# Scan steps taken in pairs, x statistics on ScalarE, the residual on ScalarE and GpSimd

## Chip, cores and metric

The kernel runs on one core of one Trainium2 chip. The metric is the device time of one execution in microseconds; the core has five engines that run their own instruction streams: TensorE (PE), VectorE (DVE), ScalarE (ACT), GpSimd (POOL) and SyncE (SP, which here only issues DMAs).

## The reference

One block of a gated cross-attention model, batch 4, 256 tokens, width 256, all in float32: a selective scan over a context, gated by the normalised x and added to x, then a mixture of 8 experts with 2 shared ones.

```python
# mixer: ctx (4,256,128) -> 256 channels, 16 states a channel
x_  = conv4(in_proj_w @ ctx); u = silu(x_ + conv_b)
dt, Bm, Cm = split(x_proj_w @ u); delta = softplus(dt_proj_w @ dt + dt_proj_b)
for t in range(256):                       # state: (b, 256, 16)
    state = state * exp(delta[t] * A) + (delta[t] * u[t]) * Bm[t]
    y[t] = sum_n state[n] * Cm[t, n]
y = (y + D * u) * silu(layernorm(x))
x = x + tanh(g_xattn) * y
# feed-forward: 2 shared experts and top 2 of 8, 176 wide each
h = layernorm(x)
x = x + tanh(g_ffn) * (shared(h) + 2.5 * sum_top2 w_e * expert_e(h))
```

## The kernel before, in words

**Tiles and steps.** A tile is 128 tokens of one batch entry: 8 tiles, numbered by `b * 2 + half`. The scan runs with channels on the partitions and tokens along the free dimension, in 64 steps of 128x512 elements: a step holds two states, two halves of the channels, 128 tokens; 8 steps make a tile. For each step `m`:
- GpSimd's `times_b(m)` (line 1021, product at 1035) makes `dbu` = delta*u times row B, into a ring of 3.
- ScalarE's `exps(m)` (673, 687) makes the decays in PSUM `psA`, a ring of 2, four instructions.
- VectorE's `scan:m` (927) runs the recurrence from `psA` and `dbu` into PSUM `psH[m % 2]`.
- VectorE's `prod:m` (937) multiplies the states with row C (`cc`, from DRAM) into `prod`, a ring of 3.
- GpSimd's `prod:m` (1083) adds it to the tile's sum `acc`. Tile 0's products are summed by TensorE instead (595).
The second half of a batch entry continues the first: `keep_ends` (915) copies each step's last column, `carry` (1058) multiplies it with the decay, `fix` (1066) adds it to the first column of `dbu` for the second half's step.

**From a tile's sum to the feed-forward.** For tiles 0 to 3 `y_sum` (TensorE) and `gate_y` (962, VectorE) give y; for tiles 4 to 7 GpSimd does it with `fold`, `fold2` and `gate_y` (1088, 1092, 1100). `to_tokens` (622) transposes on TensorE into PSUM `psD`; `residual` (970, VectorE) forms x2 = psD * gate + x in one instruction; `stats` and `variance` (VectorE 978, 984; GpSimd 1119 to 1125), `norm` (799, ScalarE), `to_features` (630, TensorE) and its copy give the tile's features. Then ten units a tile: `up` on TensorE (658, 662), `gate` on ScalarE (815) and VectorE (1009), `mul` (847, 851), `turn` and `hidden`, and `down` (534) in four groups, with `finish` (1016) last. `up:k` waits for `mul:k-2`.

**The gate of y** needs the normalised x: `z_stats` (VectorE 945, 948: bn_stats and bn_aggr; GpSimd 1106 to 1112), `z_norm` and `z_gate`.

**Order.** Every engine follows a list of tasks written out by hand (`ORDER`); nothing overtakes in a list, and semaphores tie the lists. SyncE's list issues the C rows (`rows_c`, 4 steps each), the B rows (`dt`) and, between steps 2 and 3 of the C rows, the weights (`fetch`). The B rows of batch entry 1, needed from step 16 on, are issued behind the weights.

## Time and profile before

| | |
|---|---|
| Time, median of 3 runs | 245.17 us (244.73 to 245.34) |
| Profiled execution, its own time | 245.45 us |
| Its span in the profile | 243.7 us |
| Busy: PE, DVE, ACT, POOL | 210.8, 204.2, 166.5, 185.6 us |
| Granted TensorE clock, mean | 0.965 |

The profile takes one execution. A group's mean is the duration of one instruction; where instructions of an engine follow each other they overlap a little, so that the distance between their starts is shorter than the duration. Busy time says nothing of whether an engine sets the end: for that the view by stretches and the chain of waits are read together.

### The profile page before, as it was taken

The numbers are of one execution on the slowest core, as the hardware profiler recorded it, in microseconds if no ns is written. First come the engines' busy times: TensorE is split into PE (matmuls) and PEld (weight loads), VectorE is DVE, ScalarE is ACT, GpSimd is POOL, SyncE is SP. The second block draws the span as 40 slices with busy tenths as digits, with TensorE's granted clock in tenths as the row PEclk, the third lists the DMA queues.
The fourth block names the chain that finished last, engine by engine and source line by source line (L and its number), as shares of the span: only waits on it lengthen the run. The fifth ranks groups of instructions, "written<-read, shape, count | busy, mean of one in ns | idle before, by whom it ended". The sixth has DMA issues, their size and how long they took to land.

```text
span 243.7 us, 3658 instructions
## 1 busy us (share of the span) xinstructions
PE 210.8 (87%) x854; PEld 146.8 (60%) x854; DVE 204.2 (84%) x499; ACT 166.5 (68%) x502; POOL 185.6 (76%) x227
## 2 busy tenths in 40 slices
PE   8819862958898876789997999999999999999995
PEld 4307541724566653457564767577777677676784
DVE  1887989989999999999999999999998898655320
ACT  4697998995989958767678998566674751433220
POOL 0486798999999999999999999999999767200000
PEclk9965998599999999999999999999999999999999
DMA  6687899697820320023173031203000000000000
GB/s 181 211 235 182 266 435 356 161 360 205 343 85 8 108 86 0 23 65 90 48 318 94 0 89 52 57 0 87 24 0 22 3 1 3 22 0 0 0 24 22
DMA packets 26965, 25.97 MB, mean 107 GB/s; under 512 B 1080, under 2 KB 25920, under 8 KB 26304
## 3 DMA queue, kind: packets, MB, share of 16 engines
q1 hardware_dynamic: 26656, 25.59, 32.6%
q10 hardware_dynamic: 288, 0.16, 0.2%
q8 instruction: 7, 0.11, 0.2%
q14 instruction: 14, 0.11, 0.1%
HBM read 24.56 MB, written 1.18 MB: 106 GB/s over the span
## 4 chain that ended last, share of the span: by engine, by line
PE 38%; POOL 27%; issue 13%; DMA 9%; SPq 9%; ACT 1%; DVE 1%; POOLq 0%; DVEq 0%; ACTq 0%
PE psU L662 17%; POOL acc L1083 14%; PE psD L534 12%; POOL dbu L1035 8%; DMA brows<-xdbl 6%; SPq L499 4%; DMA bb<-brows 3%; PE psM L640 3%; PE psH L541 2%; SPq L489 2%; PE psU L658 1%; POOL rs L1121 1%; SPq L492 1%; POOL dbu L1066 1%; ACT psA L687 1%
## 5 line engine op out<-in xcount | busy, mean ns | idle before, releaser
L662 PE MATMUL psU<-wup,hnT 128*128 128x352 f32 x288 | 95.2, 466 | 7.9 <-DVE hcat L851 4.3
L1035 POOL TENSOR_TENSOR dbu<-du,bb 128x512 f32<-128x512 f32 x64 | 81.5, 1290 | 4.5 <-DVE psH L927 4.0
L687 ACT ACTIVATE psA<-delta,aneg 128x127 f32<-128x127 f32 x256 | 78.1, 359 | 2.8 <-DVE psH L927 2.6
L927 DVE TENSOR_TENSOR_SCAN psH<-psA,dbu 128x512 f32<-128x512 f32 x64 | 76.7, 1219 | 2.2 <-POOL dbu L1066 1.1
L662 PEld LDWEIGHTS psU<-wup,hnT 128*128 128x128 f32 x288 | 51.6, 190 | 35.6 <-DVE hcat L851 8.8
L1083 POOL TENSOR_TENSOR acc<-acc,prod 128x512 f32<-128x512 f32 x42 | 53.6, 1275 | 4.4 <-DVE prod L937 3.0
L815 ACT ACTIVATE tg<-psU 128x176 f32<-128x176 f32 x80 | 25.0, 315 | 46.6 <-PE psU L662 46.0
L534 PE MATMUL psD<-wdn,hT 128*128 128x256 f32 x224 | 52.1, 379 | 0.0
L534 PEld LDWEIGHTS psD<-wdn,hT 128*128 128x128 f32 x224 | 41.8, 190 | 7.4
L937 DVE TENSOR_TENSOR prod<-psH,cc 128x512 f32<-128x512 f32 x64 | 42.0, 679 | 2.6 <-DMA cc<-brows 1.5
L1009 DVE SCALAR_TENSOR_TENSOR ag<-tg,psU 128x176 f32<-128x176 f32 x80 | 25.6, 330 | 15.0 <-ACT tg L815 14.5
L851 DVE SCALAR_TENSOR_TENSOR hcat<-psU,wtok,ag 128x176 f32<-128x176 f32 x64 | 24.1, 394 | 0.7
L822 ACT COPY hT<-psM 128x512 f32<-128x512 f32 (+1 forms) x32 | 16.1, 502 | 6.5 <-PE psM L640 5.9
L565 PE MATMUL psM<-ctx_sb,wk 128*128 128x256 f32 (+3 forms) x48 | 16.3, 513 | 4.2 <-DVE dnc L906 4.2
L640 PE MATMUL psM<-ident,hcat 128*128 128x128 f32 x112 | 17.6, 274 | 1.7 <-DVE hcat L851 0.9
L640 PEld LDWEIGHTS psM<-ident,hcat 128*128 128x128 f32 x112 | 13.7, 140 | 8.6 <-issue 4.4
L565 PEld LDWEIGHTS psM<-ctx_sb,wk 128*128 128x128 f32 x48 | 12.7, 270 | 7.4 <-DVE dnc L906 4.7
L658 PE MATMUL psU<-wup,hnT 128*128 128x360 f32 x32 | 11.2, 472 | 2.1 <-ACT hnT L807 2.1
L1016 DVE SCALAR_TENSOR_TENSOR outb<-psD,gates,x_sb 128x256 f32<-128x256 f32 x8 | 3.8, 476 | 7.6 <-PE psD L534 7.5
L595 PE MATMUL psD<-prod,ident 128*128 128x256 f32 x32 | 7.9, 389 | 2.4 <-DVE prod L937 2.4
L1044 POOL TENSOR_TENSOR wk<-taps,win 128x1024 f32<-128x1024 f32 x1 | 2.4, 2351 | 8.8 <-DMA taps<-in_w_taps 8.8
L1083 POOL TENSOR_TENSOR acc<-prod 128x512 f32<-128x512 f32 x7 | 8.9, 1272 | 0.0
(110 smaller groups left out, 217.1 us busy)
## 6 DMA issues: line engine op xcount, KB each, us to landing
cc<-brows SPq DMA_DIRECT2D x16, 512.0 KB, 3.9
bb<-brows SPq DMA_DIRECT2D x3, 2048.0 KB, 7.5
wup<-in_w_up SPq DMA_DIRECT2D x1, 1760.0 KB, 13.7
wdn<-in_w_down SPq DMA_DIRECT2D x1, 1664.0 KB, 16.7
wup<-in_w_up SPq DMA_DIRECT2D x1, 1408.0 KB, 8.5
x_sb<-in_x SPq DMA_DIRECT2D x4, 256.0 KB, 6.0
bb<-brows SPq DMA_DIRECT2D x1, 1024.0 KB, 6.0
out<-outb SPq DMA_DIRECT2D x8, 128.0 KB, 1.7
```

The lines of the kernel that those rows point to most:

```text
L534: last = pe.matmul(psD[:, 0:D], hT[0:m, g % HT_RING, c:c + P], wdn[0:m, f, :], start=(f == 0), stop=(f == FB - 1))
L565: last = pe.matmul(dst[:, h, back:], wk[:, DC - 1 - back, h * P:(h + 1) * P], ctx_sb[:, b, 0:L - back], start=(back == 0), stop=(back == D ...
L640: last = pe.transpose(psM[0:m, c:c + P], hcat[:, t % 2, f * P:f * P + m], ident[:, :])
L662: last = pe.matmul(dst, hnT[:, b % 2, k, lh * P:(lh + 1) * P], wup[:, j - 1, k, :], start=(k == 0), stop=(k == KT - 1))
L687: last = act.activation(dst[:, j, h, 1:], delta[:, b % 2, h, l0 + 1:l1], ACT.Exp, scale=aneg[:, h * DS + s0 + j:h * DS + s0 + j + 1])
L815: act.activation(tg[:, i % 2, :], psU[:, i % 2, 0:FF], ACT.Tanh, scale=0.5).then_inc(s_tanh, 1)
L851: last = dve.scalar_tensor_tensor(dst, up, wtok[:, b % 2, lh, j - 2:j - 1], ag[:, unit % 2, :], ALU.mult, ALU.mult)
L927: dve.tensor_tensor_scan(psH[:, i % 2], psA[:, i % DA_RING], dbu[:, i % DBU_RING], 0.0, ALU.mult, ALU.add).then_inc(s_scan, 1)
L937: dve.tensor_tensor(tile(prod[:, i % PROD_RING], i), tile(psH[:, i % 2], i), c.unsqueeze(2).broadcast_to([P, ns, EH, l1 - l0]), ALU.mult). ...
L1009: dve.scalar_tensor_tensor(ag[:, i % 2, :], tg[:, i % 2, :], 1.0, psU[:, i % 2, 0:FF], ALU.add, ALU.mult).then_inc(s_ag, 1)
L1035: pool.tensor_tensor(tile(dbu[:, m % DBU_RING], m), du[:, b % 2, :, l0:l1].unsqueeze(1).broadcast_to(shape), bb[:, b % 2, s0:s0 + ns, l0:l ...
L1083: pool.tensor_tensor(acc[:, total % 2], before, prod[:, i % PROD_RING], ALU.add).then_inc(s_add, 1)
```

## The change

Four things change, and the order of all five lists with them (SyncE's stays as it is).

- **Pairs.** `dbu`, `prod` and `acc` hold two steps a slot. One GpSimd product makes `dbu` for two steps (steps 0 and 1 singly), one VectorE product multiplies two steps' states (steps 62 and 63 singly), `keep_ends` and `fix` take two steps. The scans themselves and the decays stay single. A tile's sum is now: 1024 elements (first two pairs), 1024 (third pair), the upper half folded onto the lower (512), and two adds of 512 for the last pair.
- **x statistics.** `z_sum` (Copy with a sum as side output) and `z_square` (Square of x minus its mean, with a sum) on ScalarE, two instructions each for a batch entry, each followed by a wait for its own end; `z_mean` (one) and `z_stats` (three instead of four) on GpSimd.
- **Residual.** ScalarE copies `psD` times the gate into `ytok` in SBUF, GpSimd adds x; VectorE's instruction is gone.
- **Order.** Among others `gate_y:0` moves from behind `scan:11` to between `scan:8` and `scan:9`, and `z_stats:2` and `:3` of GpSimd move from before step 7 to steps 41 and 55.

```diff
 DA_RING, DBU_RING, PROD_RING, HT_RING = 2, 3, 3, 4
+PAIR = 2
...
+SINGLE_DBU = (0, 1)
+SINGLE_PROD = (STEPS - 2, STEPS - 1)
+def steps_of(m, single):
+    return (m, m + 1) if m in single else (m // PAIR * PAIR, m // PAIR * PAIR + PAIR)
...
     "ScalarE": """
+        load:0 project_out:0 z_sum:0 project_out:1 tanh_u:0 z_square:0 skip:0 xproj_out:0 tanh_u:1 dt_out:0
+        soft_exp:0 log_1:0 xproj_out:1 soft_log:0 z_sum:1 first:0 scan:0 dt_out:1 scan:1 soft_exp:1 log_1:1
+        scan:2 soft_log:1 z_norm:0 scan:3 scan:4 z_gate:0 project_out:2 z_square:1 tanh_u:2 scan:5 scan:6
...
     "GpSimd": """
+        z_mean:0 z_stats:0 load:0 first:0 scan:0 z_mean:1 scan:1 scan:3 scan:5 z_stats:1 scan:7 carry:0 fix:8
+        scan:9 fix:10 scan:11 carry:1 residual:0 scan:13 fix:12 fix:14 variance:0 delta0:2 delta1:2 prod:11
+        delta2:2 prod:13 scan:15 z_mean:2 prod:15 scan:17 scan:19 scan:21 scan:23 residual:1 carry:2 prod:19
...
+        carry:4 prod:35 fix:40 z_stats:2 residual:3 prod:37 variance:3 fold:4 scan:41 prod:39 fix:42 fold2:4
+        carry:5 gate_y:4 scan:43 residual:4 scan:45 fix:44 delta0:4 fix:46 delta1:4 prod:43 delta2:4 prod:45
+        variance:4 fold:5 scan:47 prod:47 fold2:5 gate_y:5 z_mean:3 scan:49 residual:5 scan:51 scan:53 z_stats:3
...
+                elif task == "z_sum":
+                    for h in range(LH):
+                        c = i * LH + h
+                        act.activation(zscrap[:, :], x_sb[:, i, h, :], ACT.Copy, accum_out=zsum[:, c:c + 1]).then_inc(s_zsum, 1)
+                        act.wait_ge(s_zsum, c + 1)
+                elif task == "z_square":
+                    act.wait_ge(s_zneg, i + 1)
+                    for h in range(LH):
+                        c = i * LH + h
+                        act.activation(zscrap[:, :], x_sb[:, i, h, :], ACT.Square, bias=zneg[:, c:c + 1],
+                                       accum_out=zsq[:, c:c + 1]).then_inc(s_zsq, 1)
+                        act.wait_ge(s_zsq, c + 1)
...
+                elif task == "residual":
+                    act.wait_ge(s_yT, i + 1)
+                    if i >= 2:
+                        act.wait_ge(s_x2, i - 1)
+                    act.activation(ytok[:, i % 2, :], psD[:, 0:D], ACT.Copy, scale=gates[:, 0:1]).then_inc(s_ytok, 1)
...
-                    if i >= PROD_RING:
-                        dve.wait_ge(*added(i - PROD_RING))
+                    if m0 >= PAIR * PROD_RING:
+                        dve.wait_ge(*added(i // PAIR * PAIR - PAIR * PROD_RING + PAIR - 1))
...
-                elif task == "z_stats":
-                    for h in range(LH):
-                        dve.bn_stats(zst[:, i * LH + h, :], x_sb[:, i, h, :]).then_inc(s_zst, 1)
...
-                elif task == "residual":
-                    dve.wait_ge(s_yT, i + 1)
-                    dve.scalar_tensor_tensor(x2[:, b, h].rearrange("p (k d) -> p k d", k=EH), psB, gates[:, 0:1],
-                                             x_sb[:, b, h].rearrange("p (k d) -> p k d", k=EH), ALU.mult,
-                                             ALU.add).then_inc(s_x2, 1)
...
-                if m >= DBU_RING:
-                    pool.wait_ge(s_scan, m - DBU_RING + 1)
+                if m >= PAIR * DBU_RING:
+                    pool.wait_ge(s_scan, m - PAIR * DBU_RING + PAIR)
...
+                    if k == 1:
+                        pool.tensor_tensor(whole, part(prod, PROD_RING, m0 - PAIR, m0), part(prod, PROD_RING, m0, m1),
+                                           ALU.add).then_inc(s_add, 1)
+                    elif k == 2:
+                        pool.wait_ge(*added(m0 - 1))
+                        pool.tensor_tensor(whole, whole, part(prod, PROD_RING, m0, m1), ALU.add).then_inc(s_add, 1)
+                        pool.wait_ge(*added(i))
+                        pool.tensor_tensor(whole[:, 0:W], whole[:, 0:W], whole[:, W:], ALU.add).then_inc(s_add, 1)
+                    else:
+                        for m in range(m0, m1):
+                            pool.wait_ge(*(added(m - 1) if m % PAIR else folded(t)))
+                            pool.tensor_tensor(whole[:, 0:W], whole[:, 0:W], part(prod, PROD_RING, m, m + 1),
+                                               ALU.add).then_inc(s_add, 1)
...
+                elif task == "residual":
+                    pool.wait_ge(s_ytok, i + 1)
+                    pool.tensor_tensor(x2[:, b, h], ytok[:, i % 2, :], x_sb[:, b, h], ALU.add).then_inc(s_x2, 1)
```

## Rows read from the trace of the kernel before

**Rows 1.** The page, busy us and share of the span of each engine.
```profile
PE 210.8 (87%) x854; PEld 146.8 (60%) x854; DVE 204.2 (84%) x499; ACT 166.5 (68%) x502; POOL 185.6 (76%) x227
```

**Rows 2.** Windows: stretch, its length, then busy us of PE, PEld, DVE, ACT, POOL.
```profile
15.60:55.90 40.30, 27.10 (x88) 19.37 (x89) 36.18 (x69) 36.46 (x104) 35.83 (x46) 0.81 0.89 292
55.90:157.40 101.50, 89.48 (x365) 60.10 (x363) 97.90 (x232) 81.57 (x249) 99.55 (x114) 1.00 0.30 97
157.40:241.00 83.60, 83.45 (x360) 61.66 (x360) 60.34 (x163) 38.65 (x125) 44.76 (x56) 1.00 0.04 14
```

**Rows 3.** Chain of waits, start us, us, what, around 157 us.
```profile
156.66 0.73 POOL yg L1100
...
157.53 0.41 PE psD L622 x2
```

**Rows 4.** Timeline of GpSimd, start us, us (a run's, if xN), what.
```profile
9.22 2.35 POOL L1044 TENSOR_TENSOR wk<-taps,win 128x1024 f32<-128x1024 f32 x1 [8.79 <-DMA taps<-in_w_taps]
...
29.25 0.22 POOL L1106 TENSOR_SCALAR zve<-zmv 128x2 f32<-128x2 f32 x1
...
30.82 1.26 POOL L1035 TENSOR_TENSOR dbu<-du,bb 128x512 f32<-128x512 f32 x1
...
55.95 3.73 POOL L1035 TENSOR_TENSOR dbu<-du,bb 128x512 f32<-128x512 f32 x3
...
93.48 0.52 POOL L1066 TENSOR_TENSOR dbu<-dbu,carry 128x4 f32<-128x4 f32 x3
...
156.66 0.72 POOL L1100 TENSOR_TENSOR yg<-acc,sz 128x256 f32<-128x256 f32 x1
...
165.76 2.69 POOL L1083 TENSOR_TENSOR acc<-acc,prod 128x512 f32<-128x512 f32 x2
```

**Rows 5.** Groups, VectorE and GpSimd: instructions, busy us, mean ns, idle before.
```profile
L937 DVE TENSOR_TENSOR prod<-psH,cc 128x512 f32<-128x512 f32 x64 | 42.0, 679 | 2.6 <-DMA cc<-brows 1.5 <-POOL acc L1083 0.9 <-issue 0.2
L915 DVE COPY ends<-psH 128x4 f32<-128x4 f32 x32 | 4.3, 149 | 0.0
L970 DVE SCALAR_TENSOR_TENSOR x_sb<-psD,gates,x_sb 128x256 f32<-128x256 f32 x8 | 3.8, 473 | 0.7 <-PE psD L622 0.7
L1035 POOL TENSOR_TENSOR dbu<-du,bb 128x512 f32<-128x512 f32 x64 | 81.5, 1290 | 4.5 <-DVE psH L927 4.0 <-DVE du L451 0.5
```

**Rows 6.** Groups on ScalarE, same columns.
```profile
L788 ACT ACTIVATE zn<-x_sb,znb,zrs 128x256 f32<-128x256 f32 x8 | 4.3, 590 | 0.0
L752 ACT ACT_TABLE_LOAD x3 | 3.8, 1283 | 0.1
L807 ACT COPY hnT<-psD 128x256 f32<-128x256 f32 x8 | 3.0, 371 | 0.9 <-PE psD L630 0.9
L810 ACT ACTIVATE psU<-psU 128x8 f32<-128x8 f32 x8 | 1.3, 157 | 4.0 <-PE psU L658 4.0
```

**Rows 7.** SyncE's issue of x's first block, landings of x, ScalarE's waits before 20 us.
```profile
2.44 0.43 SPq L462 DMA_DIRECT2D x_sb<-in_x  x1
...
DMA to landing us min/median/max: 3.7/6.0/6.1
...
ACT psM L715 <- DVE xh L889: 0.8, 1, 0.8
...
ACT uD L764 <- DVE u L899: 0.5, 1, 0.5
ACT xdbl L724 <- PE psM L575: 0.5, 1, 0.5
```

**Rows 8.** Chain of waits: the B rows of batch entry 1.
```profile
38.97 8.13 DMA brows<-xdbl
...
47.12 7.46 DMA bb<-brows
```

**Rows 9.** Chain of waits: `to_tokens:7` and `to_features:7` on TensorE.
```profile
208.40 0.22 PE psD L622 x2
...
213.13 0.31 PE psD L630 x2
```

More of the change, by code:

```diff
@@ L177 @@
+        gate:78 gate:79 hidden:30 hidden:31
     """,
     "VectorE": """
[L179 to L182 removed]
@@ L188 @@
-        keep_ends:22 log_2:3 variance:1 mul:8 mul:9 prod:21 prod:22 scan:23 keep_ends:23 prod:23 z_gate:1
-        scan:24 scan:25 finish:0 prod:24 prod:25 scan:26 scan:27 prod:26 prod:27 gate:10 route:1 mul:10 gate:11
-        gate_y:2 mul:11 scan:28 silu_u:4 prod:28 gate:12 gate:13 mul:12 mul:13 scan:29 scan:30 gate:14 prod:29
-        gate:15 mul:14 mul:15 scan:31 residual:2 gate:16 prod:30 mul:16 stats:2 prod:31 scan:32 gate:17 mul:17
-        variance:2 prod:32 scan:33 gate:18 gate:19 prod:33 keep_ends:32 keep_ends:33 gate_y:3 mul:18 mul:19
@@ L198 @@
-        prod:44 scan:45 scan:46 gate:32 gate:33 mul:32 stats:4 mul:33 prod:45 prod:46 gate:34 variance:4 mul:34
-        scan:47 gate:35 mul:35 prod:47 gate:36 finish:2 mul:36 scan:48 gate:37 mul:37 gate:38 mul:38
-        keep_ends:48 scan:49 gate:39 prod:48 mul:39 gate:40 route:4 mul:40 gate:41 mul:41 residual:5 scan:50
-        gate:42 stats:5 mul:42 gate:43 variance:5 mul:43 prod:49 keep_ends:49 z_gate:3 scan:51 prod:50 gate:44
-        gate:45 keep_ends:50 mul:44 mul:45 keep_ends:51 prod:51 scan:52 scan:53 keep_ends:52 gate:46
@@ new lines @@
+        scan:23 variance:1 keep_ends:23 prod:23 scan:24 scan:25 finish:0 prod:25 z_gate:1 scan:26 scan:27
+        prod:27 gate:10 route:1 mul:10 gate:11 gate_y:2 mul:11 scan:28 scan:29 gate:12 gate:13 mul:12 mul:13
+        prod:29 silu_u:4 scan:30 gate:14 gate:15 mul:14 mul:15 scan:31 prod:31 gate:16 gate:17 stats:2 mul:16
+        variance:2 mul:17 scan:32 scan:33 prod:33 gate_y:3 keep_ends:33 gate:18 gate:19 mul:18 mul:19 scan:34
+        scan:35 gate:20 route:2 mul:20 keep_ends:35 gate:21 prod:35 mul:21 scan:36 scan:37 gate:22 gate:23
```

309 lines of the change are left out of this document (152 added, 157 removed).

## Prediction

> **What bounds the kernel now.** I read three views in this order. The page's busy line [rows 1] shows no single full engine: PE 87%, DVE 84%, POOL 76% of the span. The windows [rows 2] show why an average misleads: from 15.6 to 55.9 us ScalarE, VectorE and GpSimd are all about 90% busy; from 55.9 to 157.4 GpSimd is busy 99.55 of 101.5 us, VectorE 97.9, while TensorE is busy only 89.5; from 157.4 to 241.0 TensorE is busy 83.45 of 83.6 us and the rest waits for it. The chain of waits [rows 3] gives the hinge: GpSimd's `gate_y:5` (starts 156.66), then `to_tokens:5` on TensorE (157.53), then nothing but TensorE up to the last `finish` at 241.0. TensorE's tasks behind `to_tokens:5` are the same in both orders, so the end moves with the end of `gate_y:5` (157.38), unless TensorE meets a new hole behind it. GpSimd sets that moment: its work from step 16's product (55.95) to `gate_y:5` is back to back [rows 4].
>
> **Price of GpSimd work.** Starts, not durations, give the cost of queued instructions. Three `dbu` products of 512 take 3.73 us, the last lasting about 1.28, so one costs (3.73-1.28)/2 = 1.23. Three `fix` of 4 elements take 0.52, 0.15 to 0.16 each. That is 0.155 us fixed and (1.227-0.155)/508 = 2.11 ns an element: 256 elements cost 0.69, 1024 cost 2.31 (the `wk` product of 1024 lasted 2.35) [rows 4]. A pair joined saves 2x1.227-2.31 = 0.147 us, only 6%. An instruction that needs its direct predecessor's result costs 0.1 to 0.2 more (two such adds took 2.69, where two free ones would take 1.23+1.28 = 2.51) [rows 4].
>
> **GpSimd from step 16 to `gate_y:5`, part by part.** Both orders hold the same steps here.
> - Products: 34 single ones become 17 pairs, 17x0.147 = -2.5.
> - Sums: tiles 2 to 5 go from 7 adds of 512 (8.59) to two of 1024 and three of 512 (8.30), 4x0.29 = -1.2; but two adds a tile now follow their own predecessor, nine in all (with tile 1's last), 9x0.15 = +1.35. Together +0.2 (from -1.2 to +0.6).
> - `fix`: 16 become 8, 8x0.155 = -1.2.
> - The residual's add is new here: `residual:1` to `residual:4`, 4x0.69 = +2.8.
> - `z_mean:2` and `z_stats:2` move in from the first stretch. The four-instruction `z_stats` took 1.57 from start to start [rows 4], three take about 1.4 with z_mean 0.2: +1.6.
> Sum: -2.5+0.2-1.2+2.8+1.6 = +0.9. The bound engine gets no lighter.
>
> The Trainium skill (GPSIMD Engine Reference, section 4.1 Engine selection) says that a two-input elementwise operation belongs on VectorE and costs about twice as much on GpSimd. The trace agrees in size: 0.69 against 0.47. By that rule alone the residual's move speaks against this change.
>
> **What it gives back.** GpSimd's own costs add up to about 100.0 us here (64 instructions of 512 by 1.227, six `delta` alike, four `variance` of four small instructions each by 1.57 like `z_stats`, 16 `fix` and 4 `carry`, and 6x0.69+0.5 for the folds and gates of tiles 4 and 5) but took 101.4: 1.4 us of stretched or late starts. With the rings now six steps deep instead of three, VectorE and GpSimd wait less for each other; I take 1.0 of the 1.4 (0 to 1.4).
>
> **VectorE** loses the residual (0.47, some 0.4 in a row), half of `keep_ends` (0.15, some 0.07 in a row) and one fixed cost of about 0.07 to 0.15 per joined `prod` [rows 5]. From step 16 to 47 that is 4x0.4+8x0.07+16x0.1 = 3.8 us, against one more gated unit (0.6). It comes off an engine that would then wait for GpSimd, so it buys nothing at the end, but covers a late start. The x statistics leave VectorE before the first scan, where it waited for ScalarE and GpSimd, and are worth nothing there.
>
> **ScalarE** gets 16 statistics instructions and 8 residual copies. The trace has no accumulating instruction. Bounds: a plain copy of 256 took 0.37, a scaled and shifted one of 256 0.59 [rows 6]; a separate accumulator read of 0.16, as the smallest activation, would make it 0.75. I take 0.6, nearer to the upper row as each waits for its own end. Before the first scan four of them (2.4 us, plus 0.3 of waiting, since x's first block lands at 2.44+3.7 = 6.1 at the earliest) stand ahead of `xproj_out:0`, where ScalarE idled 0.8+0.5+0.5 [rows 7]: the B and C rows leave 0.9 us later (0 to 1.5). Between 15.6 and 55.9 six more and `residual:0` bring 6x0.6+0.4 = 4.0 us (2.6 to 5.0) into 3.8 us of idle time [rows 2]; ScalarE just about holds.
> By the Trainium skill (ScalarE: Activation LUTs, What ACT_TABLE_LOAD costs) 256 elements cost an estimated 0.40 us with immediates and 0.49 with one pointer; with these the additions fit in the idle time, and the sum stays.
>
> **Where the stage starts.** Before, the B rows for step 16 landed at 47.12+7.46 = 54.58, and GpSimd reached the product at 55.95: 1.4 us of slack [rows 8]. GpSimd's products waited 4.0 us for scans, nearly all of it before 39 us [rows 5], as a ring of three forces; with six steps that goes, though the early `z_stats:1` and `residual:0` may take part of it. So GpSimd can arrive some 1.7 us earlier, and the landing decides: 54.6, or 55.5 with the 0.9 us of the start, as SyncE's list is the same. I take 55.5: -0.45 (-1.3 to +1).
>
> **The longer residual.** x2 now passes ScalarE (0.4) and GpSimd (0.7) instead of one VectorE instruction. `stats:i` on VectorE waits for it, with `variance:i` and the next gates behind it; on GpSimd `residual:i` waits for ScalarE with the next products behind it. Closest is `residual:4`, covered by one pair (2.31) against 0.41 for the transposes [rows 3], 0.4 for the copy and two hops. At the tail `to_features:7` comes 4.7 us after `to_tokens:7` [rows 9], and the old path filled that. New path: 0.55+0.75 and statistics at +1.45, now directly, where before `gate:65` and `mul:65` stood in front: the same 2.2 us to `variance:7`. I cost it at nothing; without that cover it is 0.7 us.
>
> **Sum.** -0.45+0.9-1.0 = -0.55 on the profiled 245.45 us (span 243.7 and 1.75 around it): 244.9. The median is 0.28 below that run: 244.6.
>
> **The rivals.**
> 1. *GpSimd bound, nothing moves much* (forecast, 0.50): 244.6, with one us around it for late starts and the landing, 243.6 to 245.9. It holds both sides of "faster".
> 2. *Waiting was the cost, not work* (0.20): B rows at 54.6 (-1.3), all 1.4 of late starts gone, dependent adds free (+0.9-1.35 = -0.45): -3.2, 242.0. For it: VectorE is as full as GpSimd. Against: GpSimd shows 0.2 us of idle.
> 3. *ScalarE becomes the bound of the first stretch* (0.22, slower). At 0.75 an accumulation it is 1.2 us short before step 16, on top of 1.5 at the start; tile 0's features, behind `z_gate:1` and its table load, arrive later and with them the gates that VectorE has between scans 16 and 19. Then GpSimd starts step 16 up to 1 us later and stalls some 2 us on `prod:19` to `prod:23`, with +0.9 of work: +3, 248. It decides from 0.65 us per accumulation. For it: ScalarE was 36.5 of 40.3 us busy [rows 2].
> 4. *Square or the accumulation doesn't run in the resident table set* (0.03): two loads of 1.28 [rows 6] around each of the last three `z_square`, some 8 us of ScalarE: +3 to +5, 249.
> 5. *A hole at the tail* (0.05): 0.7 us at `to_features:6` or `:7` each: +0.9, 245.5.
>
> **How the numbers follow.** A measurement tells about 0.3% (0.7 us) from no change, so faster is below 244.4 and slower above 245.9. Case 1 is split 0.22 faster and 0.28 same; case 2 faster; case 3 slower but 0.04; case 4 slower; case 5 0.04 same and 0.01 slower. Faster 0.42, same 0.36, slower 0.22. The range leaves out half of case 2's far end and the far ends of cases 3 and 4: 242.0 to 247.4.
>
> **What would show it.** Right: in the trace after, GpSimd is back to back from about 55.5 us, paired products start 2.3 apart, `gate_y:5` ends near 156.8 and TensorE is solid behind it; VectorE has idle time it didn't have. Wrong: a pair clearly off 2.3 us; ScalarE's `psA` groups late before 56 us with VectorE waiting for them (case 3); a table load beside `z_square` (case 4); TensorE idle in front of `to_features:6` or `:7` (case 5). The prediction fails if the first stretch moves by more than 2 us either way, since the work in the middle can't make up for it.

## The result, and the profile after

| | kernel before | changed kernel |
|---|---|---|
| median | 245.17 us (244.73 to 245.42, 5 runs) | 246.34 us (245.98 to 246.65, 5 runs) |
| profiled run | 245.45 us, span 243.7 | 245.98 us, span 243.8 |
| outside the span, profiled run | 1.75 us | 2.18 us |

The ratio of the medians is 1.0053, interval 1.0038 to 1.0068: the change is 1.2 us slower. The forecast was 244.6, faster; the time lies inside the range, on the other side of no change.

The page's busy line and the same three windows as [rows 1, 2], of the changed kernel:

```profile
PE 208.5 (86%) x854; PEld 146.0 (60%) x854; DVE 198.4 (81%) x428; ACT 177.5 (73%) x542; POOL 181.5 (74%) x174
```

```profile
15.60:55.90 40.30, 24.69 (x86) 18.14 (x86) 36.13 (x43) 37.58 (x109) 33.75 (x31) 0.76 0.86 294
55.90:157.40 101.50, 90.03 (x369) 61.23 (x369) 95.72 (x211) 84.38 (x261) 98.46 (x89) 1.00 0.29 96
157.40:241.00 83.60, 83.58 (x360) 61.23 (x358) 59.48 (x150) 43.59 (x140) 45.50 (x47) 1.00 0.04 13
```

The work went where the change sends it: VectorE is 5.8 us and GpSimd 4.1 us lighter, ScalarE 11.0 us heavier. In the middle stretch GpSimd has 3.0 us to spare where it had 2.0, VectorE 5.8 where it had 3.6, and the time didn't fall.

GpSimd's timeline of the changed kernel, start, length and, at the end of a row, idle time with its releaser; it answers to [rows 4]:

```profile
55.18 2.35 POOL L1060 TENSOR_TENSOR dbu<-du,bb 128x1024 f32<-128x1024 f32 x1
...
60.27 6.99 POOL L1060 TENSOR_TENSOR dbu<-du,bb 128x1024 f32<-128x1024 f32 x3
...
156.18 0.72 POOL L1136 TENSOR_TENSOR yg<-acc,sz 128x256 f32<-128x256 f32 x1
```

Step 16 starts at 55.18 (before: 55.95), three pairs take 6.99, so a pair is (6.99-2.35)/2 = 2.32 us, and `gate_y:5` starts at 156.18, 0.48 us sooner than before. All of this lies close to the forecast. What follows it isn't. TensorE's timeline of the changed kernel, from behind the start of `to_features:2` (107.21) to `to_tokens:5`, the rows with idle time of 0.1 us or more, and `to_tokens:5` itself:

```profile
108.17 0.63 PE L656 MATMUL psM<-ident,hcat 128*128 128x128 f32 x4 [0.53 <-DVE hcat L890]
...
131.84 1.45 PE L674 MATMUL psU<-wup,hnT 128*128 128x360 f32 x4 [0.96 <-DVE hcat L890]
...
137.40 1.45 PE L678 MATMUL psU<-wup,hnT 128*128 128x352 f32 x4 [0.54 <-DVE hcat L886]
139.02 1.45 PE L678 MATMUL psU<-wup,hnT 128*128 128x352 f32 x4 [0.17 <-DVE hcat L886]
...
155.24 0.66 PE L656 MATMUL psM<-ident,hcat 128*128 128x128 f32 x4 [0.68 <-ACT hT L861]
...
157.13 0.38 PE L638 MATMUL psD<-ident,yg 128*128 128x128 f32 x2
```

The same rows of the kernel before (`to_features:2` at 107.40), which the prediction had not looked at as a list:

```profile
124.22 0.63 PE L640 MATMUL psM<-ident,hcat 128*128 128x128 f32 x4 [0.34 <-DVE hcat L851]
132.84 0.41 PE L622 MATMUL psD<-ident,yg 128*128 128x128 f32 x2 [1.68 <-POOL yg L1100]
139.80 2.63 PE L662 MATMUL psU<-wup,hnT 128*128 128x352 f32 x8 [0.26 <-DVE hcat L847]
157.53 0.41 PE L622 MATMUL psD<-ident,yg 128*128 128x128 f32 x2 [0.53 <-POOL yg L1100]
```

Before, TensorE waited for GpSimd's `gate_y` twice, 1.68 and 0.53 us, and for VectorE's `mul` 0.34 and 0.26 us. Afterwards it waits for GpSimd not once, but 0.53, 0.96, 0.54 and 0.17 us for `mul` and 0.68 us for ScalarE's `hidden`. The waits add up to 2.81 us before and 2.88 after: they changed their owner, not their sum. The chain of waits says the same. It went through `gate_y:5` [rows 3]; the changed kernel's has no GpSimd in it near there:

```profile
154.60 0.59 ACT hT L861
155.19 0.04 issue
155.24 0.66 PE psM L656 x4
155.89 1.19 PE psU L678 x4
157.08 0.22 PE psM L656 x2
157.30 0.22 PE psD L638 x2
```

ScalarE's copy for `hidden:13`, then TensorE's own tasks one behind the other.

### The profile page after: what moved, and what is told of

The parts are those of the page before. It is cut to its first block and busy times, and to the rows that moved or that the text cites. A ratio compares the mean times of both kernels' runs of the same rounds, so it can differ in the third digit from the quotient of the medians.

```text
span 243.8 us, 3561 instructions
## 1 busy us (share of the span) xinstructions
PE 208.5 (86%) x854; PEld 146.0 (60%) x854; DVE 198.4 (81%) x428; ACT 177.5 (73%) x542; POOL 181.5 (74%) x174
## 5 line engine op out<-in xcount | busy, mean ns | idle before, releaser
L1060 POOL TENSOR_TENSOR dbu<-du,bb 128x1024 f32<-128x1024 f32 (+1 forms) x33 | 75.2, 2290 | 3.5 <-DVE du L471 2.9
L554 PE MATMUL psD<-wdn,hT 128*128 128x256 f32 x224 | 53.3, 381 | 0.5 <-ACT hT L863 0.5
L978 DVE TENSOR_TENSOR prod<-psH,cc 128x1024 f32<-128x1024 f32 (+1 forms) x33 | 39.1, 1184 | 1.1
L585 PE MATMUL psM<-ctx_sb,wk 128*128 128x256 f32 (+3 forms) x48 | 14.9, 480 | 6.2 <-DVE dnc L945 6.2
L1118 POOL TENSOR_TENSOR acc<-acc,prod 128x512 f32<-128x512 f32 x14 | 18.1, 1293 | 1.4 <-DVE prod L978 0.7
L1110 POOL TENSOR_TENSOR acc<-acc,prod 128x1024 f32<-128x1024 f32 x7 | 16.5, 2361 | 2.2 <-DVE prod L978 2.2
L1106 POOL TENSOR_TENSOR acc<-prod 128x1024 f32<-128x1024 f32 x7 | 16.5, 2357 | 1.7 <-DVE prod L978 1.7
L585 PEld LDWEIGHTS psM<-ctx_sb,wk 128*128 128x128 f32 x48 | 11.9, 254 | 8.8 <-DVE dnc L945 6.5
L646 PE MATMUL psD<-ident,hn 128*128 128x128 f32 x16 | 3.4, 296 | 7.1 <-ACT hn L838 6.5
L1112 POOL TENSOR_TENSOR acc<-acc 128x512 f32<-128x512 f32 x7 | 8.9, 1270 | 0.5
```

The source lines that it names most:

```text
L554: last = pe.matmul(psD[:, 0:D], hT[0:m, g % HT_RING, c:c + P], wdn[0:m, f, :], start=(f == 0), stop=(f == FB - 1))
L585: last = pe.matmul(dst[:, h, back:], wk[:, DC - 1 - back, h * P:(h + 1) * P], ctx_sb[:, b, 0:L - back], start=(back == 0), stop=(back == D ...
L978: dve.tensor_tensor(by_state(part(prod, PROD_RING, m0, m1)), by_state(states(m0, m1)), c.unsqueeze(2).broadcast_to([P, (m1 - m0) * NS, EH, ...
L1060: pool.tensor_tensor(by_state(part(dbu, DBU_RING, m0, m1)), du[:, b % 2, :, l0:l1].unsqueeze(1).broadcast_to(shape), bb[:, b % 2, s0:s0 + ...
```

## The experiments

Three theories were put against each other. G is the prediction's: GpSimd's work up to `gate_y:5` sets the end. H: TensorE is held by its own inputs from VectorE and ScalarE near 131 to 139 us and at 155 us. S: ScalarE's added work delays the gates or the decays. All ratios are to the kernel before, timed on the same chip; two times in us from different chips are compared by these ratios.

### Each part undone, and the rings alone

> The changed kernel with its order, but the residual back on VectorE as one instruction (placed where x's row is next used), so ScalarE's 8 copies and GpSimd's 8 adds are gone. Theory G (GpSimd's work up to gate_y:5 sets the end): five adds of 0.69 us fall away there, gate_y:5 ends 3.4 us earlier and the time is about 243.2, against 246.3 for the changed kernel. Theory H (TensorE reaches to_tokens:5 just when y is ready and is held by its own inputs at 131 to 139 us and at 155 us; GpSimd's half microsecond was not what counted): gate_y:5 ends earlier, but the time moves by half a microsecond at most, 245.8 to 246.5. Theory S (the added work of ScalarE delays gates and decays): 8 copies of 0.47 us go, about -0.7, 245.6.

`res_back` puts the residual back on VectorE as one instruction, in the new order. 248.55 us, ratio 1.0122 (1.0097 to 1.0148): 1.7 to 1.9 us slower than the changed kernel by the ratios, though GpSimd is 5.4 us lighter over the span. All three theories had expected it level or faster. TensorE has a wait of its own that the changed kernel doesn't have, shown by its timeline:

```profile
161.52 1.99 PE L552 MATMUL psD<-wdn,hT 128*128 128x256 f32 x8 [1.44 <-DVE x_sb L992]
```

`down:12` needs the accumulator bank that `residual:5` reads, and VectorE comes to it only behind a scan and a product, at 160.99. On ScalarE the copy out of the bank is an instruction of 0.47 us in a queue with gaps. So taking the residual back costs some 2 us in this order, and not through GpSimd. How much of that belongs to the place chosen for `residual:5`, behind `prod:49`, was not tried; the kernel before has it on VectorE ahead of `scan:50` with no such wait.

This run also says something of GpSimd alone. Windows from step 16's product to the start of `gate_y:5`, the kernel before, the changed kernel and `res_back` (GpSimd's busy time is the fifth: 98.77, 97.96 and 95.69 us):

```profile
55.95:156.66 100.71, 89.08 (x364) 59.98 (x363) 97.22 (x227) 80.97 (x247) 98.77 (x112) 1.00 0.30 98
55.18:156.18 101.00, 89.38 (x364) 60.44 (x364) 95.25 (x208) 84.45 (x263) 97.96 (x87) 1.00 0.30 99
55.54:157.14 101.60, 90.00 (x365) 60.49 (x364) 96.23 (x210) 83.42 (x260) 95.69 (x83) 1.00 0.30 98
```

With 2.3 us less to do than in the changed kernel, GpSimd still took 0.6 us longer, while VectorE, which has the residual back, was 1.0 us fuller; GpSimd's idle time went from 3.0 to 5.9 us. Work taken off GpSimd farther back turned into waiting there and did not bring `gate_y:5` forward.

> The changed kernel, but with the x statistics back on VectorE ahead of the first scan; z_stats of GpSimd has four instructions again at its new places. 16 accumulating instructions of 0.6 us leave ScalarE, z_mean leaves GpSimd. G: gate_y:5 about as before, -0.2, 246.1. H: -0.5 to 0, unless the holes at 131 to 139 us close. S: ScalarE is 5 us shorter before step 16, which starts no earlier (B rows), but the first features come 2 us earlier: -1.5, 244.8.

`stats_back`: 245.89 us, ratio 1.0012 (0.9994 to 1.0030), level with the kernel before. So the statistics' move to ScalarE is what makes the change slower, by 0.8 to 1.0 us by the ratios. S had forecast 1.5, H 0 to 0.5 and G 0.2. TensorE's late waits are no shorter without it (3.21 us against 2.88), so it isn't by late gates or decays there.

> Both moves undone: only the pairs and the new order stay. G: GpSimd has 5x0.69 less before gate_y:5, 242.9. H: VectorE gets 3.3 us more work while GpSimd gets less, TensorE is held by VectorE's gates: 245.3 to 246.3. S: the sum of the two other runs, 244.1. If it is faster than the kernel before (245.2) by more than 0.7 us, the pairs alone are worth having.

`pairs_only`, both undone: 247.12 us, ratio 1.0064 (1.0043 to 1.0085), with the same wait of 1.44 us for `residual:5`. It is 1.4 us faster than `res_back`, again the price of the accumulations, and no theory had it that slow (G 242.9, S 244.1, H 245.3 to 246.3).

> The kernel before with six slots instead of three for the products on GpSimd's and on VectorE's side, nothing else. My prediction counted 1.0 us for late starts that deeper rings take away. If that holds: 244.2. If GpSimd's list is full and its late starts come from elsewhere (H): within 0.3 us of 245.2.

```diff
-DA_RING, DBU_RING, PROD_RING, HT_RING = 2, 3, 3, 4
+DA_RING, DBU_RING, PROD_RING, HT_RING = 2, 6, 6, 4
```

`rings6` is the kernel before with this edit: ratio 1.0011 (0.9988 to 1.0034). Deeper rings alone give nothing, as H said: from step 16's product to `gate_y:5` it takes 100.61 us in place of 100.71.

### The order edited to close TensorE's waits

> The changed kernel once more, unaltered, timed on the chip and in the rounds of the three that follow, so that each of them has its own baseline. Nothing divides the theories here. If the first comparison holds, it is 0.3% to 0.8% above the kernel before; its time outside the span shows whether the 2.15 us of the first comparison (1.75 in the kernel before) belong to the kernel or to that chip.

Measured: 246.70 us, ratio 1.0046 (1.0024 to 1.0067), and 2.17 us outside the span in the median of 11 runs, against 1.82 for the kernel before. The difference of 0.35 us belongs to the kernel, not to a chip.

> The changed kernel with one edit in VectorE's list: log_2:4 goes ahead of gate:30, and scan:43 and prod:43 go behind mul:31 instead of standing between route:3 and mul:31. No work is added or taken away, and GpSimd's list is untouched. Theory H (TensorE is held by its own inputs near 131 to 139 us and at 155 us): mul:30 comes about 0.6 us sooner and mul:31 about 1.1 us, so the waits of 0.54 and 0.17 us that TensorE has at 137.4 and 139.0 us close; but gate_y:5 ends at 156.9 us and TensorE reaches to_tokens:5 only 0.4 us behind it, so most of the 0.7 us is lost again in a wait there: 0.2 to 0.5 us faster than the changed kernel. Theory G (GpSimd's work up to gate_y:5 sets the end): TensorE's waits before to_tokens:5 cost nothing, the same time within 0.1 us, or up to 0.5 us slower if the later scan:43 holds GpSimd's additions.

```diff
...
-scan:42 scan:43 gate:30 log_2:4 route:3 mul:30 gate:31 prod:43 mul:31
+scan:42 log_2:4 gate:30 route:3 mul:30 gate:31 mul:31 scan:43 prod:43
...
```

`order_v`: 247.70 us, ratio 1.0086 (1.0061 to 1.0112), 1 us slower than the changed kernel. The waits at 137 and 139 us are gone, and two others stand behind them: 0.99 for `hT` and 0.50 for `hcat`, since the later `scan:43` held up ScalarE's decays (0.42 us of idle time in front of the next one) and with them its copies. H had forecast 0.2 to 0.5 us faster and had the sign wrong; G had allowed up to 0.5 slower, for another reason (GpSimd's additions), and had the size wrong.

> The edit of order_v, and with it: gate:28 and to_features_out:3 sooner on ScalarE and VectorE (TensorE's wait of 0.96 us at 131.8), turn:13 ahead of up:40 and turn:14 ahead of up:41 with ScalarE's hidden:13 and hidden:14 moved to suit (the wait of 0.68 us at 155.2), and to_tokens:5 behind up:42, so that gate_y:5 may come 1.2 us later without being waited for. Again no work is added or taken away. Theory H: of the 2.35 us of waits between 131 and 156 us some 1.3 to 2.0 close, and nothing on GpSimd stands against it: 1.0 to 2.0 us faster than the changed kernel, to about 244.5. Theory G: gate_y:5 starts where it did, and to_tokens:5 comes later than it did, so the end is the same or up to 1 us later.

`order_all`: 249.92 us, ratio 1.0169 (1.0144 to 1.0194), 3.2 us above the changed kernel on the same chip, where H had forecast 1.0 to 2.0 faster. Eight waits, 4.86 us in all, three of them (0.72, 0.38, 0.56) behind 158 us, where the changed kernel has none.

> The edits of order_all on the kernel that has the statistics of x back on VectorE and the rest of the change (that kernel alone was 245.89 us, 0.4 to 0.5 us under the changed kernel). Theory S (the accumulations on ScalarE cost half a microsecond by themselves) together with H: both gains add, 0.3 to 0.6 us under order_all, about 244.0, and under the kernel before. If the accumulations cost only by the waits that the new order closes anyway, order_stats and order_all are the same within 0.2 us. G: no faster than 245.9.

`order_stats`: 247.63 us, ratio 1.0083 (1.0062 to 1.0104), 2.3 us under `order_all` though the edits are the same and the waits add up to nearly the same (4.77). S with H had forecast 0.3 to 0.6 us, and 244.0. What the accumulations cost is not in TensorE's late waits.

### Two suspects for the time outside the span, and the joining by itself

> The changed kernel with one semaphore fewer: the counter of GpSimd's negated means and that of its shifts of x, which GpSimd counts up in strict turn, become one. No instruction is added, moved or taken away. The changed kernel spends 2.17 us outside its span; the kernel before and the kernels with either half of the change undone spend 1.82. Theory O1 (those 0.35 us follow the number of semaphores, two more in the changed kernel, one more in each half): outside the span 1.8 us, and the whole 0.3 to 0.4 us faster than the changed kernel, near 246.3. Theory O2 (they belong to something else that only both halves together have): 2.17 us outside the span and the same time.

> The kernel before with two semaphores more that nothing counts up or waits for. O1: the time outside the span rises from 1.82 to about 2.17 us and the kernel is 0.3 to 0.4 us slower. O2: both stay as they are.

`sem_less` is the changed kernel with one semaphore fewer, `sems_more` the kernel before with two unused ones more. `sem_less` still spends 2.22 us outside its span (6 runs), `sems_more` still 1.81 (12 runs, ratio 1.0001, 0.9984 to 1.0018). The number of semaphores is not it. `sem_less` itself came to 1.0077 (1.0059 to 1.0096), its interval overlapping that of `after_again`.

> The changed kernel, its order and its summed pairs kept, with every product of the scan steps single again: dbu on GpSimd and the products with C on VectorE are twice as many instructions of half the width. By the trace, a pair on GpSimd is 2.31 us and a single 1.227, so some 30 splits cost GpSimd 4.4 us in all and 3.5 us up to gate_y:5; on VectorE 30 splits of 1.18 us into two of about 0.65 cost some 3 us. Theory G (GpSimd's work up to gate_y:5 sets the end): 3 to 3.5 us slower than the changed kernel. Theory H (TensorE is held by its own inputs, and GpSimd is only 0.4 us behind being waited for): the first 0.4 us is free, and VectorE's added work delays the gated units as well: 3 to 5 us slower, with waits for ag or hcat of VectorE on TensorE grown before 156 us. A rival, that joining is worth little because GpSimd's waits absorb the splits: under 1 us slower.

```diff
-SINGLE_DBU = (0, 1)
-SINGLE_PROD = (STEPS - 2, STEPS - 1)
+SINGLE_DBU = tuple(range(STEPS))
+SINGLE_PROD = tuple(range(STEPS))
...
```

The lists get the second half of each pair back, and two waits are adapted.

`singles`: 247.43 us, ratio 1.0085 (1.0068 to 1.0102), only 0.7 to 1 us slower than the changed kernel (by the medians, by the ratios), and 1.78 us outside the span, where the changed kernel has 2.17, so that within the span it is 1.1 to 1.4 us slower. GpSimd's busy time rises by 3.8 us, as the price of a pair says, but `gate_y:5` starts only 0.9 us later (1.4 us longer from step 16's product). The whole time is as the rival said, under 1 us, against 3 or more by G and H; within the span it lies just above that. Most of what joining saves on GpSimd, 3.8 us of busy time, did not reach the end.

> The kernel before, its order kept and its steps single, with the residual alone moved: ScalarE scales, GpSimd adds. Eight instructions of 0.47 us join ScalarE, eight of 0.73 us join GpSimd (5 of them before gate_y:5, 3.6 us), and eight of 0.48 us leave VectorE. Theory G: gate_y:5 comes about 3 us later and the end with it, 248 us. Theory H: the move frees VectorE and the accumulator's bank sooner, which in the changed order was worth 2 us; against that stand GpSimd's 3.6 us, which in this order is not 0.4 but 0 us from being waited for: 1 to 3 us slower. The rival that moving the residual gains by itself: 245.2 or less.

`old_res`: 263.68 us, ratio 1.0758 (1.0727 to 1.0788). Nobody expected that. A line of its waits tells it (us in total, times, longest):

```profile
POOL x_sb L1120 <- ACT ytok L805: 14.6, 6, 4.9
```

GpSimd, which has nothing to spare in that order, stood 14.6 us in six waits for ScalarE's copy, with every `dbu` product and sum queued behind. In the changed kernel, with as many residuals, the same wait is 2.8 us in two waits. Where the two halves of the residual stand in the two queues matters far more than their 0.47 and 0.73 us of work. I set those places by the times of the trace before; that the price is that of a bad place, and not of the move, is argued, since no second place was tried.

### The bound itself: two edits, four cells

> The changed kernel, with GpSimd's last two additions for half tile 5 (1.30 us each, the two ahead of fold2:5 and gate_y:5) made over 32 columns in place of 512; the rest of those two sums is left out. That takes about 2.1 us from GpSimd directly ahead of gate_y:5 and changes nothing on any other engine. Theory G (GpSimd's work up to gate_y:5 sets the end): the end comes with gate_y:5, 1.5 to 2.1 us faster than the changed kernel, 244.6 to 245.1. Theory H (TensorE's own waits set it; it reached to_tokens:5 0.08 us after gate_y:5's result): gate_y:5 starts 2 us sooner and nothing moves, 0 to 0.2 us faster.

```diff
...
-pool.tensor_tensor(whole[:, 0:W], whole[:, 0:W], part(prod, PROD_RING, m, m + 1),
+n = W // 16 if t == 5 else W
+pool.tensor_tensor(whole[:, 0:n], whole[:, 0:n], part(prod, PROD_RING, m, m + 1)[:, 0:n],
...
```

The rest of those two sums is left out.

> The changed kernel with log_2:4 and prod:43 behind mul:31 in VectorE's list (no scan is moved this time), turn:13 ahead of up:40 in TensorE's, and hidden:13 ahead of logits_out:4 and hidden:15 ahead of residual:5 in ScalarE's. GpSimd is untouched. H: TensorE's waits of 0.54, 0.17 and 0.68 us at 137.4, 139.0 and 155.2 us close or shrink, and TensorE stands at to_tokens:5 about 1 us sooner, but gate_y:5 is only 0.08 us ahead of it there: a new wait for yg of 0.8 to 1.3 us, and the end is 0 to 0.3 us sooner. G: gate_y:5 as before, the same end within 0.1 us. These two lie close; the verdict is in the pair with order_light.

```diff
...
 VectorE
-log_2:4 route:3 mul:30 gate:31 prod:43 mul:31
+route:3 mul:30 gate:31 mul:31 log_2:4 prod:43
 TensorE
-up:39 up:40 turn:13 turn:14 up:41
+up:39 turn:13 up:40 turn:14 up:41
...
```

On ScalarE `hidden:13` goes ahead of `logits_out:4` and `hidden:15` ahead of `residual:5`.

> Both edits at once: the order of order_w and GpSimd's two short additions of light_after. H: neither alone gains, both together 0.8 to 1.5 us against the changed kernel, about 245.2, since now neither TensorE nor GpSimd holds to_tokens:5. G: as light_after alone, 1.5 to 2.1 us, and order_w adds nothing to it. If the end falls under neither edit and not under both, what holds it lies behind to_tokens:5, and H falls too.

| | GpSimd as changed | GpSimd 2 us lighter |
|---|---|---|
| order as changed | 246.70, 1.0046 (`after_again`) | 246.64, 1.0056 (`light_after`) |
| order of `order_w` | 247.93, 1.0110 | 247.95, 1.0096 |

The changed kernel's line of the two additions, and three of `light_after`, where they take 0.59 us together:

```profile
152.69 2.61 POOL L1118 TENSOR_TENSOR acc<-acc,prod 128x512 f32<-128x512 f32 x2
```

```profile
154.12 0.59 POOL L1119 TENSOR_TENSOR acc<-acc,prod 128x32 f32<-128x32 f32 x2
...
155.59 0.72 POOL L1137 TENSOR_TENSOR yg<-acc,sz 128x256 f32<-128x256 f32 x1
...
156.66 0.66 PE L656 MATMUL psM<-ident,hcat 128*128 128x128 f32 x4 [0.68 <-ACT hT L861]
```

(In this profile everything from the first stretch on stands 1.4 us later than in the changed kernel's; 155.59 is 2.0 us sooner relative to it.) `gate_y:5` is 2 us sooner, TensorE's waits are the same five to 0.01 us, and the end hasn't moved. G is refuted for the changed kernel. `order_w` changed only which wait stands where: the transposes of `turn:10` need a bank that `log_2:4` reads, so moving `log_2:4` back opened a wait of 1.60 us:

```profile
138.46 0.66 PE L658 MATMUL psM<-ident,hcat 128*128 128x128 f32 x4 [1.60 <-DVE dnc L947]
```

and the lighter GpSimd was no use there either. The expectation of `order_light` had said that H falls too if the end falls under neither edit and not under both. It did not fall: both cells of the second row are 1.2 to 1.3 us up. TensorE's waits in them add up to 3.98 and 3.97 us, against 2.88, so the case that was meant, TensorE ahead of time and GpSimd light, never came about. H's forecasts failed each time, and no experiment closed a wait and gained by it.

What is left of H is a sum. TensorE has the same list of matmuls from `to_features:2` to the last `finish` in every kernel, so at one clock that stretch should be a constant plus its waits; that much is bookkeeping, and the question is how well it holds. From each profile, the stretch (start of `to_features:2` to start of the last `finish`) less the sum of the waits of 0.1 us or more in it:

| kernel | stretch | waits | rest |
|---|---|---|---|
| before | 133.62 | 2.81 | 130.81 |
| rings6 | 133.32 | 2.47 | 130.85 |
| changed | 133.95 | 2.88 | 131.07 |
| light_after | 133.97 | 2.89 | 131.08 |
| order_w / order_light | 134.95 / 134.94 | 3.98 / 3.97 | 130.97 |
| order_v | 134.92 | 3.67 | 131.25 |
| stats_back | 134.57 | 3.21 | 131.36 |
| res_back | 135.84 | 4.24 | 131.60 |
| singles | 135.65 | 3.61 | 132.04 |
| order_all | 136.72 | 4.86 | 131.86 |
| pad | 133.77 | 2.89 | 130.88 |
| pairs_only | 135.63 | 4.24 | 131.39 |
| order_stats | 136.75 | 4.77 | 131.98 |
| old_res | 147.92 | 11.49 | 136.43 |

Apart from `old_res` the rest stays within 1.2 us while the stretch varies by 3.4. GpSimd's busy time over the span varies in these from 176.1 (`res_back`) to 185.6 (before) and doesn't order them at all. In `old_res` the rest is 5 us longer: TensorE's granted clock is 0.93 between 130 and 150 us, 0.98 from there to 166 and 0.89 between 200 and 230, and (1-0.93)x20+(1-0.98)x16+(1-0.89)x30 = 5.0 us, as an estimate, is what the lower clock took; it is 1.00 in the three windows under `res_back`. The table does not say why the changed kernel is slower: of its 0.33 us over the kernel before, 0.07 are waits.

> The changed kernel with 16 memsets of one column each at the end of VectorE's first task, at 4.6 us, where VectorE waits 0.95 us for ScalarE anyway. The kernels with 2.17 us outside the span are those whose VectorE program is the shortest (428 instructions in the profile), those with 1.82 have 436 and more. If the time outside the span follows that length, it falls to 1.8 us here and the whole by 0.2 to 0.4 us; if not, it stays at 2.17 and the kernel is the same or up to 0.5 us slower.

```diff
+SPARE = 16
...
+for k in range(SPARE):
+    dve.memset(spare[:, k:k + 1], 0.0)
```

`pad`: 246.25 us, ratio 1.0050 (1.0030 to 1.0070), and 1.83 us outside the span, where the changed kernel has 2.17 and on this same chip `order_w` has 2.17 and `light_after` 2.18. Sixteen instructions more took 0.35 us away from the time outside the span. In the whole time that is not clear of the noise (`light_after` 246.64, `pad` 246.25, their ratios' intervals overlap). Every kernel here with 428 VectorE instructions has 2.15 to 2.22, every one with 436 or more has 1.78 to 1.84. So it goes with the length of VectorE's program, or with something that changes along with it; by what mechanism stays open.

### The first stretch

> The changed kernel with the statistics of x back on VectorE, and with project:3 ahead of to_features:0 in TensorE's list and to_features_out:0 ahead of z_norm:1 and z_gate:1 in ScalarE's, so that the product for the third quarter runs in the 6.5 us in which TensorE waits for hn, and up:0 can start near 48 to 50 us where it started at 53.2. If the first stretch counts through TensorE, the end comes 1 us or more sooner than in stats_back (245.89, 1.0012 times the kernel before), near 245. If TensorE's later waits for VectorE (1.72 us at 57.5, and the one for gate_y:2 at 107.2) take the gain up again, the same within 0.3 us.

> The same two moves on the changed kernel itself with the 16 small memsets of pad, and z_sum:0 behind tanh_u:0 and z_square:0 behind xproj_out:0 on ScalarE, so that ScalarE's project_out:1 no longer stands behind its wait for x (0.29 us at 5.73 in the changed kernel, 0.66 us in a profile where x came later). If that wait and the stretch behind it are what the move of the statistics costs, this comes down to early_stats within 0.2 us and 0.3 to 0.5 us under pad (246.25); if not, it stays at pad's 1.005 times the kernel before.

```diff
...
 TensorE
-to_tokens:0 to_features:0 project:3 up:0
+to_tokens:0 project:3 to_features:0 up:0
 ScalarE
-norm:0 scan:12 z_norm:1 scan:13 scan:14 z_gate:1 to_features_out:0
+norm:0 scan:12 to_features_out:0 z_norm:1 scan:13 scan:14 z_gate:1
...
```

`early_stats`: 249.87 us, ratio 1.0174 (1.0149 to 1.0199); `early_pad`: 251.19 us, ratio 1.0243 (1.0215 to 1.0271). In `early_stats` `up:0` did start 3.8 us sooner, at 49.44, and the time came out 4.0 us above `stats_back`; `early_pad` is 4.9 us above `pad`. Both expectations failed. TensorE's timeline of `stats_back` and then of `early_stats` shows the same twelve matmuls of `up:2` to `up:4`:

```profile
57.56 4.12 PE L677 MATMUL psU<-wup,hnT 128*128 128x352 f32 x12 [1.72 <-DVE hcat L869]
```

```profile
58.61 6.25 PE L677 MATMUL psU<-wup,hnT 128*128 128x352 f32 x12 [6.54 <-DVE hcat L869]
```

With `project:3` out of the way TensorE ran into one unbroken wait of 6.54 us, and came out of it at half clock. The windows of `early_stats` (the number behind the busy times is the granted clock):

```profile
53.00:57.50 4.50, 0.00 (x0) 0.00 (x0) 3.27 (x9) 4.49 (x14) 4.28 (x4) 0.91 1.12 313
57.50:61.00 3.50, 2.39 (x4) 1.51 (x5) 2.68 (x10) 1.11 (x4) 3.42 (x3) 0.50 0.51 124
61.00:65.00 4.00, 4.00 (x10) 2.12 (x9) 2.24 (x6) 2.52 (x9) 3.17 (x2) 0.68 0.00 0
```

In `stats_back` the clock is 1.00 in all three; its own stretch at 0.50, 46.57 to 51 us, lies under `project:3`, ahead of `up:0`. Of the 3.2 us by which `to_tokens:1` is late (71.60 against 68.43), 1.05 is the later start of `up:2` and 6.25-4.12 = 2.1 is the clock. So the experiment changed more than it meant to, and does not say what an earlier `up:0` is worth at full clock. It does say that a delay in the first stretch goes through to the end nearly whole (3.14 us at the last `finish`). And it says something of the wait for x. In `early_pad` ScalarE no longer waits for x, both kernels have 1.83 us outside the span, and still the one with the statistics on ScalarE is 1.3 us slower (251.19 against 249.87, same chip).

## Why the prediction was wrong, step by step

**The start of the stage and GpSimd's sum came out nearly right, the sum by luck.** Step 16 was put at 55.5 and started at 55.18. From there to `gate_y:5` the forecast was 100.71+0.9-1.0 = 100.6 us, and 101.00 was measured. `gate_y:5` was to move by -0.55 and moved by -0.48. A pair was to cost 2.31 from start to start, measured 2.32; the residual's add was priced at 0.69 from start to start and lasts 0.73. But the two terms of the sum were +0.9 of work and -1.0 of late starts given back, and the windows under `res_back` show neither: GpSimd's busy time fell by 0.8 us (98.77 to 97.96) and its idle time rose by 1.1 (1.9 to 3.0). Two wrong terms cancelled as the two measured ones do. That rival 1's outcome on GpSimd, nearly no change, came true didn't help, because GpSimd was no longer the one to wait for.

**The step that failed** is the first paragraph's "the end moves with the end of `gate_y:5` (157.38), unless TensorE meets a new hole behind it". It took the chain of waits, which passes from GpSimd to TensorE at `to_tokens:5`, as proof that GpSimd set the end, and looked for new holes only behind it. How long TensorE had waited there it did not read: 0.53 us. A faster GpSimd could bring that and no more, and ahead of `to_tokens:5` the new order put waits for VectorE and ScalarE (0.96+0.54+0.17+0.68) in place of GpSimd's 1.68 and 0.53. `light_after` shows it directly: 2 us off GpSimd, nothing at the end. `res_back` shows it for the sentence "GpSimd sets that moment": 2.3 us less work, and `gate_y:5` 0.6 us later from step 16 on. `rings6` shows it for the 1.0 us of "late starts given back": 0.1 us from step 16 to `gate_y:5`, and a ratio of 1.0011.

**The account of the profiled run.** Forecast 244.9, measured 245.98, 1.08 too low. Time outside the span, taken as unchanged: 2.18-1.75 = 0.43 (`pad` returns 0.35 of it). From `to_tokens:5` to the last `finish`, taken as unchanged: 241.16-157.13 = 84.03 against 241.02-157.53 = 83.49, so 0.54. It is 84.03 to 84.05 in all five other profiles of kernels with the changed kernel's statistics and residual and its order behind 157 us (`after_again`, `sem_less`, `light_after`, `pad`, `order_v`), and 83.49 to 83.54 in `before`, `sems_more` and `rings6`, so it belongs to the order. One place can be named on the chain of waits: eight `down` matmuls at 192.00 take 1.99 us where the others take 1.73. `gate_y:5` 0.07 later than forecast, and `to_tokens:5` following it by 0.95 where it was 0.87: another 0.15. That is 1.12 of 1.08.

**The median** is 1.7 above the forecast, since the profiled run of the kernel before, 245.45, lies above all five timed ones and that of the changed kernel is its fastest. That accounts for the remaining 0.64 us (0.28 and 0.36) by the choice of the runs, and the runs differ by their first stretch: `to_features:2` starts anywhere from 107.2 to 108.8 us in the profiles of the changed kernel and its near copies, and from 107.1 to 108.1 in `before`, `sems_more` and `rings6`. In that stretch rival 3 was half right. Four pairs of kernels differ by the statistics' place: `stats_back` and the changed kernel (0.8 to 1.0 us), `pairs_only` and `res_back` (1.4), `order_stats` and `order_all` (2.3), `early_stats` and `early_pad` (1.3). In the first and the third 0.35 us of it lie outside the span, in the other two nothing does. The place is not rival 3's, though. Groups on ScalarE in the changed kernel, count, busy us and mean ns:

```profile
L811 ACT ACTIVATE zscrap<-x_sb,zneg 128x256 f32<-128x256 f32 x8 | 4.0, 505 | 0.1
L805 ACT ACTIVATE zscrap<-x_sb 128x256 f32<-128x256 f32 x8 | 3.3, 415 | 0.4 <-DMA x_sb<-in_x 0.3
L805 ACT ACTIVATION_READ_ACCUMULATOR zscrap<-x_sb 128x1 f32 x8 | 1.5, 190 | 0.0
```

An accumulation is 0.54 us from start to start for the sum and 0.63 for the square, under the 0.65 from which rival 3 decided. The B and C rows left 0.14 us later, not 0.9: the idle time of [rows 7] took nearly all of it. What stands in the first stretch is the wait for x (0.29 us at 5.73 in this profile, 0.66 in that of `sem_less`) and, at 29.20, GpSimd's wait of 3.98 us for `z_square:1` in ScalarE's queue with the next `dbu` products behind it, a wait the prediction named in half a sentence and did not price. The two rows, ScalarE's and GpSimd's, of the changed kernel:

```profile
5.73 0.42 ACT L805 ACTIVATE zscrap<-x_sb 128x256 f32<-128x256 f32 x1 [0.29 <-DMA x_sb<-in_x]
```

```profile
29.20 0.19 POOL L1146 TENSOR_SCALAR zve<-zsq 128x2 f32<-128x2 f32 x1 [3.98 <-ACT zscrap L811]
```

With the statistics on VectorE (`stats_back`) GpSimd has two other, shorter waits there:

```profile
29.11 2.37 POOL L1053 TENSOR_TENSOR dbu<-du,bb 128x1024 f32<-128x1024 f32 x1 [1.68 <-DVE du L470]
32.84 0.22 POOL L1076 TENSOR_TENSOR carry<-ends,dec 128x16 f32<-128x16 f32 x1 [1.36 <-ACT dec L789]
```

The traces tell the two suspects apart. Three starts in each: GpSimd's first product, its first product behind `carry:0`, and TensorE's `to_features:2`.

| kernel | first product | behind `carry:0` | apart | from there to `to_features:2` |
|---|---|---|---|---|
| changed | 15.62 | 33.30 | 17.7 | 73.9 |
| pad | 16.01 | 33.97 | 18.0 | 73.9 |
| light_after | 16.02 | 34.65 | 18.6 | 74.0 |
| sem_less | 16.01 | 34.93 | 18.9 | 73.9 |
| stats_back | 16.21 | 33.40 | 17.2 | 73.8 |
| pairs_only | 16.08 | 32.98 | 16.9 | 73.8 |
| order_stats | 15.91 | 32.33 | 16.4 | 73.8 |

From that product on nothing differs: the last column is 73.8 to 74.2 in all 13 profiles of kernels with pairs and the changed kernel's order there. The first product is no later with the statistics on ScalarE (15.6 to 16.2 us in ten profiles) than with them on VectorE (15.9 to 16.2 in three), so the wait for x doesn't carry it. Between the two products it is 17.7 to 18.9 us in the ten and 16.4 to 17.2 in the three, and there the wait for `z_square:1` stands, 3.97 to 4.94 us long in the ten. Its length also makes most of the spread between runs: 3.98 in the changed kernel's profile, 4.94 in that of `sem_less`. No run moved `z_square:1` alone, so the place is shown by traces and not by an experiment.

The Trainium skill (ScalarE: Activation LUTs, What ACT_TABLE_LOAD costs) gave 0.40 and 0.49 us as estimates for these activations; the trace has 0.415 and 0.505 for them, but the accumulator is read by a second instruction of 0.19 us that the estimate leaves out.

**The longer residual,** of which the prediction says "I cost it at nothing", did better than the one alternative that was run: `res_back` is nearly 2 us slower. The prediction looked at who waits for x2, and not at who waits for the bank that the residual reads. `residual:5` on VectorE, in the place it had in `res_back`, holds `down:12` for 1.44 us. The Trainium skill (GPSIMD Engine Reference, section 4.1 Engine selection) would keep such an add on VectorE, as about twice as slow on GpSimd. The instructions here took 0.73 us on GpSimd and 0.47 on VectorE, a factor of 1.55, so the prediction's "agrees in size" was too kind. In this order the split was the better choice even so, because the copy frees the bank from another queue; against a better place on VectorE no run compares it.

**Rivals 4 and 5** did not occur: no table load stands beside `z_square`, and TensorE has no wait in front of `to_features:6` or `:7`.

No version of the change that was tried beats the kernel before. The nearest is `stats_back` with 1.0012 (0.9994 to 1.0030).

## What to carry to other kernels

Before taking an engine as the bound, list all waits of the engine that runs last, not only the one on the chain, and see how far behind the second cause stands: here it was half a microsecond, so nothing done to GpSimd alone could bring more. A busy share of 97% is no proof either: with less work GpSimd stood idle for longer and came no sooner. The quickest test is to leave 2 us of work out on the suspected engine directly ahead of the hinge. When an instruction is moved to another engine, price what its operand's buffer holds up, and where in the new queue it will wait; its own duration is the smaller part.
